# Self-attention in a fused decoder layer: exponentials kept in their PSUM bank until VectorE has scaled them

## The reference

```python
x = x + tanh(g_xattn) * cross_attention(layernorm(x), ctx)           # 16 heads of 128, 361 context rows
h = rms(layernorm(x)); q, k = rope(h @ wq + bq, h @ wk + bk); v = h @ wv + bv
scores = where(causal, q k^T / sqrt(32), min)                        # 16 heads of 32, 100 x 100 per batch
ctx = softmax(scores) @ v;  y = layernorm(x) + ctx @ wo
y = y + top-2-of-8 experts(rms(y)) + gated shared MLP(rms(y))
x = x + tanh(g_ffn) * y
```

## Time and profile before

| | us |
|---|---|
| median of 3 runs | 926.47 (923.95 to 930.01) |
| the profiled execution | 930.65 |
| its span | 928.9 |
| PE busy | 899.1 (97%) |
| DVE busy | 646.2 (70%) |
| ACT busy | 560.9 (60%) |
| POOL busy | 322.0 (35%) |

### The profile page before, as it was taken

One profiled execution on the slowest core, in us unless ns is written; L12 is line 12 of the kernel. 1 busy time (PEld: TensorE's weight loads), 2 busy tenths in 40 slices (PEclk: granted clock), 3 DMA queues, 4 the chain that ended last, 5 costly groups with the idle time before them and its releaser, 6 DMA issues.

```text
span 928.9 us, 16126 instructions
## 1 busy us (share of the span) xinstructions
PE 899.1 (97%) x5713; PEld 837.1 (90%) x5713; DVE 646.2 (70%) x1482; ACT 560.9 (60%) x1448; POOL 322.0 (35%) x344
## 2 busy tenths in 40 slices
PE   8989999999999999999999999899999999999996
PEld 7989999999999999999987878799999999999996
DVE  3547777774446778784286985848585988897863
ACT  3656667664555666674433766745436787877851
POOL 3432222335552223234653542335400133323221
PEclk8989999999999999999999999999999999999999
DMA  5732730005550000002542121124338999999975
GB/s 155 221 93 79 220 94 1 1 12 169 153 163 24 17 1 1 1 12 66 149 124 78 58 59 47 51 57 124 112 101 285 300 322 312 317 304 329 310 191 153
DMA packets 112760, 122.20 MB, mean 132 GB/s; under 512 B 9887, under 2 KB 77927, under 8 KB 112680
## 3 DMA queue, kind: packets, MB, share of 16 engines
q1 hardware_dynamic: 97806, 98.80, 34.2%
q0 software_dynamic: 5184, 12.13, 5.9%
q10 hardware_dynamic: 9690, 10.24, 3.9%
HBM read 110.72 MB, written 19.07 MB: 140 GB/s over the span
## 4 chain that ended last, share of the span: by engine, by line
PE 65%; DVE 16%; DMA 9%; ACT 4%; issue 4%; POOL 1%; ACTq 0%; SPq 0%; DVEq 0%
PE bank L2078 59%; DMA eraw<-in_L_ffn_w_gate_e_dram 6%; PE bank L2225 4%; DVE we L1356 2%; DVE wf L1356 1%; ACT we L928 1%; DVE sm L1587 1%; DMA sums<-s_sum 1%; DMA raw<-s_unit 1%; DMA raw<-in_L_xattn_Wq_dram 1%; DMA X<-in_x_dram 1%; DVE TE L1786 1%; DVE PQ L1563 1%; DVE stat L1623 1%; DVE PQ L1561 1%
## 5 line engine op out<-in xcount | busy, mean ns | idle before, releaser
L1947 POOL TENSOR_SCALAR SC<-SC,mx,anyv 100x361 f32<-100x361 f32 x128 | 82.0, 651 | 205.3 <-DVE mx L1463 191.9
L1356 DVE TENSOR_TENSOR we<-eraw,we 128x704 fp32r<-128x704 f32 (+2 forms) x140 | 107.3, 802 | 24.7 <-ACT we L928 24.4
L928 ACT ACTIVATE we<-eraw 128x704 fp32r<-128x704 f32 (+2 forms) x140 | 96.7, 718 | 37.6 <-DMA eraw<-in_L_ffn_w_gate_e_dram 21.5
L1930 POOL TENSOR_TENSOR wx<-raw,wx 128x512 fp32r<-128x512 f32 x64 | 83.3, 1310 | 76.6 <-ACT wx L914 76.3
L1930 POOL TENSOR_TENSOR wf<-raw,wf 128x512 fp32r<-128x512 f32 x54 | 71.6, 1333 | 103.6 <-ACT wf L914 103.5
L2078 PE MATMUL bank<-H2h,wf 128*128 128x400 f32 x352 | 100.2, 351 | 0.0
L1045 ACT ACTIVATE SC<-SC,mx 100x361 f32<-100x361 f32 x128 | 75.4, 594 | 19.9 <-DVE mx L1476 19.5
L2078 PE MATMUL bank<-XTh,wx 128*128 128x400 f32 x256 | 71.6, 353 | 0.7 <-POOL wx L1930 0.7
L2078 PE MATMUL bank<-QOh,wx 128*128 128x400 f32 x256 | 70.9, 348 | 1.0 <-DVE mx L1476 1.0
L2008 POOL DMA_INDIRECT XB<-s_h,inv x20 | 21.9, 1094 | 143.4 <-PE bank L2524 113.3
L914 ACT ACTIVATE wf<-raw 128x512 fp32r<-128x512 f32 x100 | 61.6, 628 | 15.0 <-DMA raw<-s_unit 7.2
(11 more groups left out here) (289 smaller groups left out, 2672.3 us busy)
## 6 DMA issues: line engine op xcount, KB each, us to landing
raw<-s_unit SPq DMA_DIRECT2D x60, 256.0 KB, 3.6
eraw<-in_L_ffn_w_gate_e_dram SPq DMA_DIRECT2D x40, 352.0 KB, 4.6
eraw<-in_L_ffn_w_up_e_dram SPq DMA_DIRECT2D x40, 352.0 KB, 5.2
eraw<-in_L_ffn_w_down_e_dram SPq DMA_DIRECT2D x40, 256.0 KB, 5.4
raw<-in_L_xattn_Wq_dram SPq DMA_DIRECT2D x32, 256.0 KB, 2.9
raw<-in_L_xattn_Wo_dram SPq DMA_DIRECT2D x32, 256.0 KB, 2.8
eraw<-in_L_ffn_w_down_e_dram SPq DMA_DIRECT2D x20, 192.0 KB, 5.2
s_unit<-in_L_ffn_w_sh_gate_dram SPq DMA_DIRECT2D x11, 256.0 KB, 3.7
```

Source lines behind the costliest of these rows:

```text
L928: eng.activation(weights("e", u)[0:rows, 0, 0:n], eraw[u % 6][0:rows, 0:n], ACT.Copy).then_inc(sem("act_e"), 1)
L1356: return eng.tensor_tensor(o, src, f32(hi), ALU.subtract)
L1930: eng.tensor_tensor(w[:, 1, :, :], raw[plan.raw[stream, u] % 4][:, :, :], f32(w[:, 0, :, :]), ALU.subtract).then_inc(sem("pool_w"), 1)
L1947: eng.tensor_scalar(sc, sc, m[:, 3, h:h + 1], anyv[:, b:b + 1], ALU.mult, ALU.mult).then_inc(sem("pool_p"), 1)
```

## The change

For the units 0 to 21 the exponentials are written back into the score bank that they are read from. DVE scales them from the bank into `PF`. The wait for a free `PF` tile (transposes of unit u-4 done) moves from ACT's exponentials to DVE's scaling. Since the bank now holds the exponentials until they are scaled, `f_scores` waits for the scaling of its two former units rather than for their exponentials, in the steps 2, 4, ... 22. For units 22 to 31 nothing changes but the form of the wait. No instruction is added, taken away or put elsewhere in a queue.

```diff
             if u < 32:
                 act.wait_ge(sem("dve_fn"), u + 1)
-                if u >= 4:
+                if u >= 4 and u in BY_POOL:
                     act.wait_ge(sem("pe_ft"), u - 3)
                 p, m, bank = PF[u % 4], sm[u % 4], score_bank[u % 4]
                 for c in range(4):
-                    e = eng.activation(p[:, c, :], bank[0:T, c * T:(c + 1) * T], ACT.Exp, bias=m[:, 1, c:c + 1],
+                    sc = bank[0:T, c * T:(c + 1) * T]
+                    e = eng.activation(p[:, c, :] if u in BY_POOL else sc, sc, ACT.Exp, bias=m[:, 1, c:c + 1],
                                        scale=-1.0, accum_out=m[:, 2, c:c + 1])
...
                     chained(eng.reciprocal(m[:, 3, :], m[:, 2, :]))
+                    if u >= 4:
+                        dve.wait_ge(sem("pe_ft"), u - 3)
                     r4 = m[:, 3, :].rearrange("p (a o) -> p a o", o=1).broadcast_to([T, 4, T])
-                    eng.tensor_tensor(p[:, :, :], p[:, :, :], r4, ALU.mult).then_inc(sem("dve_fp"), 1)
+                    src = score_bank[u % 4][0:T, 0:4 * T].rearrange("p (a b) -> p a b", a=4)
+                    eng.tensor_tensor(p[:, :, :], src, r4, ALU.mult).then_inc(sem("dve_fp"), 1)
...
             if q:
-                pe.wait_ge(sem("act_fe"), 4 * q - 2 + 2 * pair)
+                for i in strips:
+                    u = 4 * q - 4 + i
+                    name, value = ("act_fe", u + 1) if u in BY_POOL else plan.scaled(u)
+                    pe.wait_ge(sem(name), value)
```

## The result

The changed kernel takes 946.17 us (median of 6 runs, 941.97 to 948.09), the kernel before 926.24 (median of 6, 923.95 to 930.01). The recorded ratio is 1.0205, interval 1.0182 to 1.0228 (the two medians divided give 1.0215): 19 to 20 us slower. The forecast was 945.3, range 935 to 956. In the experiments too a ratio can differ by 0.001 from that of the medians. The profiled execution of the changed kernel took 944.07 us, with a span of 942.3.

What follows compares the result with a forecast made beforehand. PE was taken to bound the kernel, with DVE as full up to 550 us. Stalls of 6.0 + 0.8 + 3.0 + 2.2 = 12.0 us and 6.8 us of clock, on 926.47, gave 945.3 us, range 935 to 956.

Steps and rivals of the forecast that it cites:

- The chain of 1.5 us: In even steps PE's scores wait for its own transposes, then DVE's copy, reciprocal and scaling: 1.5 us later.
- Step 2: The scores wait for the scaling of unit 1, started at 515.02 and ended at 515.59: a 1.5 us stall.
- Steps 14, 16, 20, 22: PE did not wait there before and DVE has slack: 1.5 us of stall each, 6.0 us together.
- Step 18: Scores already wait for ACT until 565.51; the scaling ends at 566.28, so 0.8 us is added.
- Steps 2 and 4: Scores wait for the scaling of units 1 and 3; DVE catches up to 1.5 us each, together 3.0 us.
- Steps 6 to 12: Four stalls of 1.5 us replace PE's present waits for DVE or ACT: 2.2 us taken, bounds 1 and 4.
- The clock: PE's stalls make the granted clock fall to half: two falls taken, 6.8 us; none to six possible, 0 to 20 us.
- Stalls alone: Rival: PE's stalls cost 12 us and the clock holds: 938.5 us, range 935 to 942; chance 0.28.
- Mostly hidden: Rival: DVE's relief and old waits absorb steps 2 to 12; only steps 14 to 22 pay 6.8 us: 933; chance 0.07.
- the contention does not go: Rival: POOL still holds up the scaling from PSUM, 4 us more than the forecast, 949 us; chance 0.02.
- Faster: Rival: scaling sets the pace up to 550, its contention all on the path: -4.6 us, or 922; chance 0.03.
- step 22 at 590 if the clock held: Sign: step-22 scores, at 578.7 before, start at 590, and 3 us later for each half-clock stretch.

Runs made afterwards that it cites:

- experiment 5: The changed kernel with the change applied to units 0 to 13 alone, the other units as before: 937.11 us, ratio 1.0108.
- Experiment 1: The changed kernel with DVE's copy of the transposed unit to PTf moved behind the scaling in even steps: 929.68 us, ratio 1.0014 to the kernel before.
- the second: Second profile of the changed kernel, unedited, beside new runs of the kernel before: 946.07 us, ratio 1.0187; the profiled execution took 947.94 us.
- experiment 4: The changed kernel with four idle matmuls, results unused, between transposes and scores in each even step 4 to 22: 941.97 us, ratio 1.0154 to the kernel before.
- experiment 3: The changed kernel with the change applied to units 14 to 21 alone, units 0 to 13 as before: 938.09 us, ratio 1.0118 to the kernel before.
- experiment 7: The kernel before with the scaling replaced by a maximum over the same SBUF tile, one operand instead of two: 923.70 us, ratio 0.9962.

## Why the prediction was right

- **What bounds.** The delay went to the end in full: 15.4 us up to step 22, 1.1 more behind it. DVE's fullness in the first half did not hide it (experiment 5).
- **The chain of 1.5 us.** Listed as 1.45 us in nine of eleven places, and in eight of them it is the chain that was predicted. Experiment 1 shows it causally: one block moved in DVE's queue gives 18 us back, the same waits kept. That DVE's copy stands ahead of the scaling was the step on which the sum hung.
- **Step 2 was luck.** The prediction speaks of "the 1.5 us that the structure sets" there, but there is no copy in step 2. Its 1.45 us come of a late DVE, and experiment 1 left them standing. The number was read from rows of the kernel before and held; the reason given for it did not.
- **The terms.** Steps 14, 16, 20, 22: 5.8 in place of 6.0. Step 18: 0.9 (1.32 less 0.41) in place of 0.8. Steps 2 and 4: 2.9 in place of 3.0. Steps 6 to 12: 4.9 less 2.2, so 2.7, in place of 2.2. Sum 12.3 in place of 12.0.
- **Steps 6 to 12 in detail.** "Four stalls of 1.5" was three of 1.45 and one of 0.54 in step 6. PE has fillers ahead of the scores there, and the wait for DVE runs beside them.
- **No price for the PSUM operand.** The scaling took 574 ns, against 575 from SBUF. The Trainium skill, VectorE: DVE Perf Modes, section on the TRN2 errata, would have it 65 ns longer; the trace does not agree. With 22 x 574 ns in place of a mean of 785, the 4.6 us left DVE's scaling as predicted, and DVE never stood before it, so the moved wait for a free `PF` tile cost nothing. The exponential, left open between 335 and 399 ns, became cheaper:

```profile
L1140 ACT ACTIVATE bank<-bank,sm x88: 305/322/361, 505.9 to 588.4; 100x100 f32<-100x100 f32 x88
```

- **The clock.** This term came out right by luck. It was two falls of 6.9 us, 3.4 us each. In the first profile there were two falls, but each of 3.4 us, and they cost 3.1 us together; in the second five, which cost 7.2. A fall was worth 1.4 to 1.6 us, less than half of the price taken, and there were up to five of them. The medians leave 6.5 us beside the 12.3 and the 1.1 behind step 22, and the fillers of experiment 4 gave back 4 us with one fall left. A single row carried both number and size. Its other row, 2.36 of 3.40 us with no fall behind it, separates nothing: in experiment 3 the clock fell in the same step, behind a like stretch of 2.37.
- **The rivals.** "Stalls alone", 938.5, is what a clock that holds would have given. Experiment 4 bears it out: 13.8 us over the kernel before, with one fall left, is about 12.2 without it. "Mostly hidden" is refuted by experiment 5, "the contention does not go" by the 576 ns. "Faster" had one half right: the contention was mostly on the path of the kernel before (3.5 us, experiment 7). Its condition, a scaling that is done before PE reaches its scores, did not hold.
- **Slips.** The lowest terms of "stalls alone" add up to 926.5 + 6.8 + 4.0 = 937.3, not to the 935 that its range begins with. The sign "step 22 at 590 if the clock held" was met, by 590.97, although the clock fell twice: the first scores came 3.1 us earlier, as much as the two falls cost. Only the distance from first scores to step 22, 87.10 us, says what happened.

## What to carry to other kernels

When a wait is moved to a later event on another engine, look at what stands ahead of that event in its engine's queue in the same step. Here it was a copy that itself waited for the waiting engine, so a hand-over of 0.7 us of work became a round trip of 1.5 us in eight of eleven even steps, and moving the copy behind the scaling brought them to 0.74 us or less. Where TensorE bounds, price such stalls twice: once as their time (12.3 us here), once as half-clock time behind them (3 to 7 us here), and take the second as a range.

## What the runs showed of the hardware

- Two SBUF operands against one. In the same place a scaling with both in SBUF took up to 1474 ns beside POOL work, with one in PSUM 573 to 576, and a reduction with one in SBUF 569 to 571. The Trainium skill, SBUF — State Buffer, section Who interferes with whom, states it so: a VectorE instruction with two SBUF inputs contends with a GpSimd instruction that reads SBUF, and one with at most one, outside the modes that use both ports, does not. The trace agrees. The rotary products, which keep two SBUF inputs, still took up to 1.54 us beside POOL work in these steps of the changed kernel, where their median is 574 to 575 ns.
- ScalarE's exponential of 100 x 100 takes 322 ns into PSUM and 347 into SBUF (medians), from PSUM in both. The Trainium skill, ScalarE: Activation LUTs, section Step-by-step: what each stage is for, calls PSUM the lower-latency destination; the trace agrees, with 25 ns.
- The granted clock fell behind some stalls and not behind others that look alike. Ahead of both falls of the first profile PE was busy 2.08 and 1.95 of 3.40 us, and around step 16, with no fall behind it, 1.95 too:

```profile
511.30:514.70 3.40, 2.08 (x22) 1.71 (x23) 3.30 (x8) 2.43 (x11) 3.19 (x3) 1.00 0.15 49
579.60:583.00 3.40, 1.95 (x23) 1.38 (x22) 2.66 (x7) 2.25 (x10) 1.07 (x1) 1.00 0.26 77
...
563.40:566.80 3.40, 1.95 (x24) 1.34 (x22) 2.97 (x8) 1.23 (x8) 0.00 (x0) 1.00 0.00 0
```

A fall also came where PE had been busy 2.37 of 3.40 us (experiment 3). Which stall is followed by a fall was not settled, and two executions of the same program differ in it.
